# Experts' rows added to the output by the scatter itself, and the tail's scatters interleaved with its gathers

## The reference

```
ys   = y / sqrt(512);  d = rsqrt(einsum(ys*ys, w*w) + eps)
xf   = ((x * ys) @ w_cond) * d                       # modulated projection
top1 = argmax(softmax(xf @ gate_w.T))                # 2 experts, one per token
routed = sum_e (relu(masked_e(xf) @ w1[e] + b1[e]) @ w2[e] + b2[e])
         # masked_e zeroes the tokens of the other expert, so each token also gets
         # the other expert's constant row relu(b1) @ w2 + b2
shared = relu(xf @ sw1 + sb1) @ sw2 + sb2            # hidden size 2048
out    = x + routed + shared
```

## Time and profile before

| what | value |
|---|---|
| median of 3 runs | 1483.02 us |
| the profiled execution | 1490.29 us, of which the span from first to last instruction is 1488.5 us |
| TensorE busy in the span | 1475.4 us, 99% |
| VectorE, ScalarE, GpSimd busy | 748.4, 455.4, 310.8 us |
| mean granted TensorE clock | 0.997 |

### The profile page before, as it was taken

One profiled execution on the slowest core, in us unless ns is written; L12 is line 12 of the kernel. 1 busy time (PEld: TensorE's weight loads), 2 busy tenths in 40 slices (PEclk: granted clock), 3 DMA queues, 4 the chain that ended last, 5 costly groups with the idle time before them and its releaser, 6 DMA issues.

```text
span 1488.5 us, 17699 instructions
## 1 busy us (share of the span) xinstructions
PE 1475.4 (99%) x6502; PEld 1219.7 (82%) x6502; DVE 748.4 (50%) x1151; ACT 455.4 (31%) x724; POOL 310.8 (21%) x354
## 2 busy tenths in 40 slices
PE   9999999999999999999999999999999999999996
PEld 8888888888888888888888888888888888888885
DVE  7854523444438868685944515233274523315242
ACT  4343332324335444443523211112133211211112
POOL 0000233120001100000131331515234051523404
PEclk9999999999999999999999999999999999999998
DMA  6947675686678998886764220202135020211203
GB/s 205 282 150 206 228 224 205 182 246 226 217 278 305 284 282 261 281 246 198 234 200 128 70 72 8 83 23 70 42 103 177 21 83 25 66 47 33 79 0 89
DMA packets 157572, 229.17 MB, mean 154 GB/s; under 512 B 46720, under 2 KB 63616, under 8 KB 157504
## 3 DMA queue, kind: packets, MB, share of 16 engines
q1 hardware_dynamic: 142496, 190.90, 40.2%
q0 software_dynamic: 15008, 37.37, 8.9%
HBM read 143.78 MB, written 85.49 MB: 154 GB/s over the span
## 4 chain that ended last, share of the span: by engine, by line
PE 98%; another core or an unknown queue 1%; DVE 0%; issue 0%; ACT 0%; POOL 0%; DVEq 0%; ACTq 0%; POOLq 0%
PE bank L1624 23%; PE bank L1713 23%; PE bank L1694 23%; PE bank L1659 20%; PE bank L1570 6%; PE bank L1748 1%; PE bank L1771 1%; PE bank L1547 0%; PE bank L1553 0%; PE bank L1758 0%; DVE hl L1172 0%; POOL out L674 0%; ACT hf L967 0%; DVE aux L1323 0%
## 5 line engine op out<-in xcount | busy, mean ns | idle before, releaser
L1624 PE MATMUL bank<-xw,w_hi 128*128 128x512 f32 x1024 | 315.1, 389 | 0.0
L662 POOL DMA_INDIRECT rows_e<-xf_scratch,soft x144 | 142.0, 986 | 762.4 <-DVE xe_lo L1359 442.9
L1659 PE MATMUL bank<-hl,w_hi 128*128 128x512 f32 x896 | 276.1, 389 | 0.3
L940 ACT ACTIVATE hf<-bank,b 128x512 f32<-128x512 f32 x128 | 88.3, 690 | 556.6 <-PE bank L1694 434.5
L1477 DVE CAST h_hi<-hf 128x512 fp32r<-128x512 f32 x128 | 55.3, 432 | 376.4 <-ACT hf L940 302.8
L1624 PEld LDWEIGHTS bank<-xw,w_hi 128*128 128x128 f32 x1024 | 192.1, 188 | 39.7
L1694 PE MATMUL bank<-xe_hi,w_hi 128*128 128x512 f32 x512 | 199.4, 389 | 0.1
L1694 PE MATMUL bank<-xe_lo,w_hi 128*128 128x512 f32 x512 | 199.2, 389 | 0.0
L1624 PE MATMUL bank<-xw,w_lo 128*128 128x512 f32 x512 | 199.2, 389 | 0.0
L1713 PE MATMUL bank<-w_hi,h_hi 128*128 128x512 f32 x512 | 199.2, 389 | 0.0
L1713 PE MATMUL bank<-w_lo,h_hi 128*128 128x512 f32 x512 | 199.2, 389 | 0.0
(11 more groups left out here) (185 smaller groups left out, 1566.9 us busy)
## 6 DMA issues: line engine op xcount, KB each, us to landing
hin<-hidden_scratch SPq DMA_DIRECT2D x112, 512.0 KB
hidden_scratch<-vt SPq DMA_DIRECT2D x64, 512.0 KB, 3.7
hidden_scratch<-vb SPq DMA_DIRECT2D x48, 512.0 KB
stage<-w_pack SPq DMA_DIRECT2D x64, 256.0 KB
raw<-w_shared SPq DMA_DIRECT2D x44, 256.0 KB, 3.7
ring<-x_cols SPq DMA_DIRECT2D x32, 256.0 KB, 4.6
xf_scratch<-xo SPq DMA_DIRECT2D x32, 256.0 KB, 4.2
rows<-xf_scratch SPq DMA_DIRECT2D x16, 512.0 KB, 9.5
```

Of the source, the lines that this page charges most:

```text
L662: pool.indirect_dma_start(rows_e[:, c % JN, :], None, xf_dram, bass.IndirectOffsetOnAxis(tab_rows[:, c:c + 1], 0)).then_inc(rows_gathered, ...
L940: nc.scalar.activation(hf[:, j % 2, :], h_ps[j % 2][:], ACT.Relu, bias=b1[:, 1 + e, j:j + 1]).then_inc(hf_ready, 4)
L1624: last = nc.tensor.matmul(turn[c][p][:], w[:, 2 * h + q, 2 * g + p, part], xw[:, 2 * t + q, x, k, :], start=(n == 1), stop=(n == 12))
L1659: last = nc.tensor.matmul(bank[p][:], w[:, DOWN_W[c], i, part], hl[:, n % HL, h, :], start=(i == 0 and q == 0), stop=(i == PAIRS - 1 and q ...
```

## The change

The shared rows are stored straight into `out`. The scratch tensor and the gather of shared rows are gone. The scatter carries `compute_op=ALU.add`, so that the DMA adds `res` to the rows that `out` already holds. `res` now is the product in PSUM plus `xr` (x row and bias), so VectorE's addition of `xr` to `res` is gone too. In the tail each of the four steps u = 32 to 35 now waits for `out_ready`, scatters unit u-4, gathers the x rows of unit u, waits until that scatter has landed and raises `rows_landed` by one.

```diff
         def part_rows(s, half, side, q):
-            return part_dram[t0:t0 + T, q * QF + side * 64:...]
+            return out[t0:t0 + T, q * QF + side * 64:...]
...
-            def gather_res(u):
-                pool.indirect_dma_start(res[:, u % W, :], None, part_dram,
-                                        bass.IndirectOffsetOnAxis(tab_in[:, u:u + 1], 0)).then_inc(res_gathered[u % W], DMA)
...
             def scatter(u):
                 pool.indirect_dma_start(out, bass.IndirectOffsetOnAxis(tab[:, u:u + 1], 0), res[:, u % W, :], None,
-                                        bounds_check=N - 1, oob_is_err=False).then_inc(scattered, DMA)
+                                        bounds_check=N - 1, oob_is_err=False, compute_op=ALU.add).then_inc(scattered, DMA)
...
                 gather_xr(u)
                 if u >= W:
                     pool.wait_ge(scattered, DMA * (u - W + 1))
-                gather_res(u)
                 rows_done(u + W)
...
-            pool.memset(spare[:, COLS:COLS + 1], 0.0).then_inc(rows_landed, W)
-            for u in range(NT - W, NT):
-                pool.wait_ge(out_ready, u + 1)
-                scatter(u)
             for u in range(NT, UNITS_E):
+                pool.wait_ge(out_ready, u - W + 1)
+                scatter(u - W)
                 gather_xr(u)
-            pool.wait_ge(scattered, DMA * NT)
-            for u in range(NT, UNITS_E):
-                gather_res(u)
+                pool.wait_ge(scattered, DMA * (u - W + 1))
+                pool.memset(spare[:, u + W:u + W + 1], 0.0).then_inc(rows_landed, 1)
             for u in (*range(NT + 1, UNITS_E), NT):
-                pool.wait_ge(res_gathered[u % W], 2 * DMA * up_to(u, u % W))
+                pool.wait_ge(xr_gathered[u % W], DMA * up_to(u, u % W))
                 if u == NT:
                     pool.wait_ge(out_ready, u + 1)
...
-                nc.vector.tensor_tensor(res[:, part, :], res[:, part, :], xr[:, part, :], ALU.add).then_inc(res_ready, W // 2)
...
-                    last = nc.vector.tensor_tensor(res[:, m, :], y_ps[m][:], res[:, m, :], ALU.add)
+                    last = nc.vector.tensor_tensor(res[:, m, :], y_ps[m][:], xr[:, m, :], ALU.add)
```

More of the change, by code:

```diff
@@ L122, in build @@
     hid_dram = nc.dram_tensor("hidden_scratch", (BLOCKS * UNITS * P, T), F32).ap()
-    part_dram = nc.dram_tensor("partial_scratch", (N, D), F32).ap()
     table_dram = nc.dram_tensor("token_table", (COLS * P, IDW), I32).ap()
@@ L170, in build @@
         tab_in = sb("tab_in", [P, COLS], I32)
-        spare = sb("spare", [P, COLS + W])
+        spare = sb("spare", [P, COLS + 2 * W])
         def tiles(w, cols):
@@ L262, in build @@
         rows_landed = sem("rows_landed")
-        res_gathered = [sem(f"res_gathered{i}") for i in range(W)]
+        xr_gathered = [sem(f"xr_gathered{i}") for i in range(W)]
         consts_made = sem("consts_made")
@@ L352, in build @@
         y_mm = sem("y_mm")
-        xr_biased = sem("xr_biased")
-        res_ready = sem("res_ready")
+        xr_ready = sem("xr_ready")
         out_ready = sem("out_ready")
@@ L391, in part_rows @@
             t0 = (2 * s + half) * T
-            return part_dram[t0:t0 + T, q * QF + side * 64:q * QF + side * 64 + 64].rearrange("(j b) f -> b j f", b=B32)
+            return out[t0:t0 + T, q * QF + side * 64:q * QF + side * 64 + 64].rearrange("(j b) f -> b j f", b=B32)
         def turned(k0, k1, j0, j1):
@@ L666, in gather_xr @@
                 pool.indirect_dma_start(xr[:, u % W, :], None, x_rows,
-                                        bass.IndirectOffsetOnAxis(tab_in[:, u:u + 1], 0)).then_inc(res_gathered[u % W], DMA)
-            def gather_res(u):
-                pool.indirect_dma_start(res[:, u % W, :], None, part_dram,
-                                        bass.IndirectOffsetOnAxis(tab_in[:, u:u + 1], 0)).then_inc(res_gathered[u % W], DMA)
+                                        bass.IndirectOffsetOnAxis(tab_in[:, u:u + 1], 0)).then_inc(xr_gathered[u % W], DMA)
             def scatter(u):
                 pool.indirect_dma_start(out, bass.IndirectOffsetOnAxis(tab[:, u:u + 1], 0), res[:, u % W, :], None,
-                                        bounds_check=N - 1, oob_is_err=False).then_inc(scattered, DMA)
+                                        bounds_check=N - 1, oob_is_err=False, compute_op=ALU.add).then_inc(scattered, DMA)
             def rows_done(u):
@@ L727, in _ @@
                     wait_apart(pool, out_ready, tail[u - NT - 1], tail_ready)
-                    pool.memset(spare[:, COLS + u - NT:COLS + u - NT + 1], 0.0)
+                    pool.memset(spare[:, u + 2 * W:u + 2 * W + 1], 0.0)
                 scatter(u)
@@ L1449, in add_bias @@
                 for i in range(W):
-                    dve.wait_ge(res_gathered[i], 2 * DMA * up_to(u + W - 1, i))
+                    dve.wait_ge(xr_gathered[i], DMA * up_to(u + W - 1, i))
                 part = slice(half * W // 2, (half + 1) * W // 2)
                 nc.vector.tensor_tensor(xr[:, part, :], xr[:, part, :], bias[:, e:e + 1, :].broadcast_to([P, W // 2, D]),
-                                        ALU.add).then_inc(xr_biased, W // 2)
-                dve.wait_ge(xr_biased, u + (half + 1) * W // 2)
-                nc.vector.tensor_tensor(res[:, part, :], res[:, part, :], xr[:, part, :], ALU.add).then_inc(res_ready, W // 2)
+                                        ALU.add).then_inc(xr_ready, W // 2)
             def add_bias_unit(u, e):
                 for i in range(W):
-                    dve.wait_ge(res_gathered[i], 2 * DMA * up_to(u, i))
+                    dve.wait_ge(xr_gathered[i], DMA * up_to(u, i))
                 part = bass.ds(u % W, 1)
-                nc.vector.tensor_tensor(xr[:, part, :], xr[:, part, :], bias[:, e:e + 1, :], ALU.add).then_inc(xr_biased, 1)
-                dve.wait_ge(xr_biased, u + 1)
-                nc.vector.tensor_tensor(res[:, part, :], res[:, part, :], xr[:, part, :], ALU.add).then_inc(res_ready, 1)
+                nc.vector.tensor_tensor(xr[:, part, :], xr[:, part, :], bias[:, e:e + 1, :], ALU.add).then_inc(xr_ready, 1)
             def keep_unit(u, n):
@@ L1490, in wide_slot @@
                 dve.wait_ge(y_mm, HC * (u + W))
-                dve.wait_ge(res_ready, u + W)
+                dve.wait_ge(xr_ready, u + W)
                 for m in range(W):
-                    last = nc.vector.tensor_tensor(res[:, m, :], y_ps[m][:], res[:, m, :], ALU.add)
+                    last = nc.vector.tensor_tensor(res[:, m, :], y_ps[m][:], xr[:, m, :], ALU.add)
                 last.then_inc(out_ready, W)
@@ L1511, in unit_slot @@
                 dve.wait_ge(y_mm, HC * (u + 1))
-                dve.wait_ge(res_ready, u + 1)
+                dve.wait_ge(xr_ready, u + 1)
                 part = bass.ds(u % W, 1)
-                nc.vector.tensor_tensor(res[:, part, :], y_ps[0][:].unsqueeze(1), res[:, part, :], ALU.add).then_inc(out_ready, 1)
+                nc.vector.tensor_tensor(res[:, part, :], y_ps[0][:].unsqueeze(1), xr[:, part, :], ALU.add).then_inc(out_ready, 1)
             def change(e):
```

## The result

The changed kernel takes 1491.19 us (median of 5 runs, 1490.68 to 1491.44), the kernel before beside it 1483.30: ratio 1.0054, 95% interval 1.004 to 1.0069. It is slower by 7.9 us. The forecast was 1484.1, no change that can be measured; the time lies outside the range too.

What follows compares the result with a forecast made beforehand. TensorE was taken to bound the kernel, leaving only the last 39 us to answer. GpSimd's later list (+0.3) and the last landing (+0.8) made +1.1 on the median 1483.02: 1484.1 us, range 1482.6 to 1489.0.

Steps and rivals of the forecast that it cites:

- What bounds the kernel: Wide slots: TensorE never waits there, so work taken from GpSimd, VectorE or DMA gives 0; only the last 39 us can answer.
- The repair of the profiled tail: Tail: ScalarE's profiled hole taken out as absent from unprofiled runs; sum 1483.05 against median 1483.02, 7.25 us below the profiled execution.
- x: What one adding scatter takes longer than a plain one, issue to landing: 1.0 us taken, bounds 0 and 2.0.
- The prediction's own sign of being wrong: Steps of four in the tail of GpSimd's list above 4.7 us would show rival B.
- this rule: Two source reads per chunk run at half a copy's rate: x would be 0.7 and the sum 1483.6.
- The step's own length: Each of four new tail steps on GpSimd's list: 3.3 + x us, including 0.12 memset and a 0.2 gap.
- The padding scatters: Tail, after the four steps: three padding scatters with their memsets take 5.1 us, as before.
- The last landing: End of the tail: the last scatter lands 0.8 us later, as it carries fewer than 128 rows.
- rival B: Tail, slower: four landings in a row decide, each us of x counting four times; 1488.9 at x = 2.0; chance 0.32.
- x = 1.39: Value of x from which rival B's tail loss passes 2.97 us (0.2%), the smallest change a measurement can tell.
- 4.8x - 3.7: Rival B's change in us, four tail steps plus 0.8x for the last landing; +5.9 at x = 2.0.

Runs made afterwards that it cites:

- before_again: The kernel before, unchanged, run once more for one profile: span 1480.3 us in an execution of 1482.14 us.
- half_row: The changed kernel with the adding scatter taking only the first 256 features of each row, half of each routed row missing: 1485.82 us, ratio 1.0023 to before.
- plain_spread: The changed kernel without the scatter's addition, new tail order kept, shared expert's rows lost: 1482.18 us, ratio 0.9995 to before.
- add_nopad: The changed kernel without the scatters of units 33 to 35, which hold only padding, and their waits and memsets: 1484.96 us, ratio 1.0015 to before.
- add_batch: The changed kernel with adding scatters kept but the tail's old order, four scatters back to back and one wait: 1483.51 us, ratio 1.0007 to before.
- plain_batch: The changed kernel without the scatter's addition and with the tail's old order, shared rows lost: 1481.62 us, ratio 0.9994 to before.

## Why the prediction was wrong

**What bounds the kernel: right.** TensorE's rows in the wide slots didn't move, and taking a gather, 256 KB and an addition out of each step gave nothing. VectorE's 18.8 us less busy time and GpSimd's 13.8 don't appear in the time.

**The repair of the profiled tail: right.** VectorE's last addition was put at 1474.3; it is at 1473.71 in before_again and 1474.22 in the changed kernel. The span was put at 1481.25 and was 1480.3; that the sum met the median to 0.03 us was closer than the method is, so partly luck. Without this step the profile of before would have given over 7 us of slack in which the new tail would have seemed free.

**x, the price of an adding scatter: this step failed.** It was put at 1.0, by the row of a gather, with a lower end of 0 and an upper end of 2.0. It is 4.9 - 2.8 = 2.1, of which 0.57 is issue: above the upper end too. The prediction's own sign of being wrong came, steps above 4.7 us: they were 5.6 to 6.2. Two things were wrong in the choice. The issue was taken to be 0.1 longer because gather and scatter issue alike; but both are copies, and say nothing of an operation that reads two places. And the read was put beside the write as if each moved at a copy's pace; half_row gives 2.2 us for the adding transfer against 0.7. The Trainium skill, "Collectives: The Full Stack", section on the bandwidth ceiling, has two reads per chunk and half the rate in a reduce-scatter among cores; the direction is borne out, the size is not: the transfer is three times as long here, and the page says nothing of the issue. The time that the prediction gave for this rule, 1483.6, doesn't follow from its own terms either: with x = 0.7 the list is free at 1475.4, before VectorE's side at 1475.85, and -0.45 + 0.8 x 0.7 gives 1483.1.

**The step's own length: too short by 0.3.** From memset to the next scatter 0.2 was taken; in the tail the idle time there is 0.68 to 0.94, as the earlier trace rows had it before the first padding scatter (0.68). The wait before it was taken a little too long, so 0.3 a step is left: the first step of plain_spread, without the addition, needs 3.60 and not 3.3 (its later ones still more), and four steps of the changed kernel take 1476.43 - 1453.77 = 22.7, not 4 x (3.3 + 2.1) = 21.6.

**The padding scatters: too short by 1.1.** The 5.1 us of before were kept; from 1476.43 until the third was issued at 1482.61 they took 6.2, as each is an adding scatter too, with 1.55 of issue and nothing to move. add_nopad measures what they are worth on this list: 5.5.

**The last landing:** +0.8 was taken; the last scatter's start to the end of the span is 6.6 us against 4.9 in before_again, so +1.7. That is 0.8 of the measured x, so the fraction was right and x was not. add_batch and plain_batch differ by 1.9 us and in little else.

**The mechanism was in the prediction, as rival B**, with the right place, the right factor of four and the right point from which it decides (x = 1.39), and 0.32. With the measured x its own line 4.8x - 3.7 gives +6.4. Steps and padding add 1.1 each; the kernel before releases its last scatter at 1475.4, 0.9 sooner than its repaired tail; and the list started 0.3 sooner than assumed: 6.4 + 2.2 + 0.9 - 0.3 = 9.2, which is what the spans of the two profiles differ by (1489.5 - 1480.3). The medians differ by 7.9, and the kernel before itself had medians between 1482.35 and 1483.30 beside the various runs, so the sum can't be held against the times more closely than about 1 us. What made the range too short is that its upper end was the upper bound of x with every other term at its middle. The other terms of the list were taken from rows of plain scatters too, and erred the same way.

**What stays open:** why the adding transfer takes three times as long rather than twice; and what held ScalarE for 9 us in one profile.

## What to carry to other kernels

Before a wait for a landing is put between DMAs that had none, count how often that landing then lies in a row, and multiply its uncertainty by that number: with the same adding scatters the kernel was 0.9 us above the kernel before when four were issued back to back and waited for once, and 7.9 when each waited for the one before. An operation that the trace doesn't show is better priced at its upper bound where it stands in a chain, since rows of simpler operations bound it from one side only; here even that bound, 2.0, was passed. And a profiled execution that lies 7 us above the median should be repaired by hand, or taken again, before slack is read off it.

## What the runs showed of the hardware

An indirect scatter with addition of 128 rows of 2 KB took mostly 1.55 to 1.60 us to issue (up to 1.99 in the tails) against 1.01, also where all rows were dropped by the bounds check, and 4.8 to 4.9 us from issue to landing against 2.8; with rows of 1 KB 3.8, with all rows dropped 2.7 against 2.1. Four of them issued 1.87 us apart landed 2.1 to 2.3 us apart (add_batch), so their issue and the fixed 1.1 us of the landing overlap with the transfer of the one before, and the transfers don't overlap with each other.
